# A decoder layer on one core: queries' operands laid out by pairs of heads, maxima issued first at two places, and a context turned by the sync queue

## What is computed

```
x = LN(x + causal_attention(x))            # 16 heads of 16
x = LN(x + slot_attention(x, context))     # see below
x = LN(x + top-4-of-16 experts(x))         # experts of 64

def slot_attention(slots, P):              # 256 slots, 256 rows of context
    Pn = rmsnorm(P, input_norm_w)
    k, v = Pn @ Wk.T, Pn @ Wv.T
    for _ in range(3):
        q = rmsnorm(slots, slot_norm_w) @ Wq.T
        attn = softmax(q @ k.T / 16, axis=slots)
        attn = attn / (attn.sum(-1) + eps)
        slots = gru_cell(attn @ v, slots)
    return slots
```

## Time and profile before

| | us |
|---|---|
| median of 3 runs | 668.17 (667.05 to 669.31) |
| the profiled execution | 666.62 |
| its span in the trace | 664.9 |

### The profile page before, as it was taken

How to read it: one execution, slowest core, us unless ns; L and a number is a source line. 1 busy time by engine, 2 the same in 40 slices (tenths; PEclk the granted TensorE clock), 3 DMA queues, 4 the chain that set the end, 5 groups by cost and what they waited for, 6 DMA issues and landing times.

```text
span 664.9 us, 13964 instructions
## 1 busy us (share of the span) xinstructions
PE 621.7 (93%) x5064; PEld 565.3 (85%) x5064; DVE 493.7 (74%) x1039; ACT 327.0 (49%) x734; POOL 225.2 (34%) x274
## 2 busy tenths in 40 slices
PE   5988998998999999999999999999999998899996
PEld 4766787776767989999899998999989988799996
DVE  4755474674764788879888799887999888767653
ACT  5444553553575355655556555565566644231320
POOL 9402332432453251422223232232312213352543
PEclk9799898997999999999999999999999999999999
DMA  8634646357400040010000000000000000042240
GB/s 283 203 103 146 173 135 190 93 173 217 121 18 1 1 160 0 2 33 2 0 0 0 32 0 0 0 0 0 0 1 1 1 1 1 16 147 82 80 157 34
DMA packets 31374, 43.34 MB, mean 65 GB/s; under 512 B 3072, under 2 KB 18912, under 8 KB 31328
## 3 DMA queue, kind: packets, MB, share of 16 engines
q1 hardware_dynamic: 31328, 42.73, 21.1%
HBM read 29.39 MB, written 13.21 MB: 64 GB/s over the span
## 4 chain that ended last, share of the span: by engine, by line
PE 56%; DVE 13%; issue 13%; DMA 5%; SPq 5%; POOL 4%; ACT 3%; DVEq 0%; POOLq 0%; ACTq 0%
PE bank L448 26%; PE bank L2171 11%; PE bank L1991 4%; POOL hid_hl L801 3%; DMA k_rows<-k_hl 3%; PE bank L1891 2%; DMA q_op<-negT 2%; PE bank L1977 1%; PE bank L456 1%; PE bank L1849 1%; PE bank L2008 1%; SPq L519 1%; PE bank L1856 1%; PE bank L1872 1%; PE bank L2000 1%
## 5 line engine op out<-in xcount | busy, mean ns | idle before, releaser
L448 PE MATMUL bank<-slots_hl,whhT_hl 128*128 128x256 f32 x864 | 113.1, 284 | 0.0
L448 PEld LDWEIGHTS bank<-slots_hl,whhT_hl 128*128 128x128 f32 x864 | 105.5, 188 | 2.4 <-ACT gate_z L1104 1.0
L1293 DVE TENSOR_REDUCE neg_max<-bank 128x2 f32<-128x512 f32 (+1 forms) x96 | 65.7, 690 | 55.2 <-PE bank L1858 41.3
L2171 PE MATMUL bank<-attn_hl,vg_hl 128*128 128x256 f32 x864 | 105.7, 280 | 0.1
L2171 PEld LDWEIGHTS bank<-attn_hl,vg_hl 128*128 128x128 f32 x864 | 100.9, 188 | 4.3 <-ACT attn_hl L815 3.9
L870 ACT ACTIVATE pT<-bank 128x512 f32<-128x512 f32 x96 | 56.9, 598 | 57.7 <-PE bank L1872 41.7
L682 POOL TENSOR_SCALAR_AFFINE_SELECT pT<-pT 128x512 f32<-128x512 f32 x64 | 40.6, 638 | 117.5 <-ACT pT L870 117.4
L696 POOL TENSOR_TENSOR sq<-sq 128x256 f32<-128x256 f32 x24 | 18.1, 754 | 170.6 <-ACT sq L1089 130.3
L801 POOL TENSOR_TENSOR hid_hl<-hid,hid_hl 128x512 fp32r<-128x512 f32 x32 | 40.9, 1303 | 25.8 <-ACT hid_hl L815 25.7
L448 PE MATMUL bank<-x2T_hl,keys_hl 128*128 128x256 f32 x384 | 48.6, 284 | 0.0
L448 PE MATMUL bank<-values_hl,hid_hl 128*128 128x256 f32 x384 | 47.8, 281 | 0.3 <-DVE x L1567 0.3
(11 more groups left out here) (212 smaller groups left out, 1298.2 us busy)
## 6 DMA issues: line engine op xcount, KB each, us to landing
gate_rows<-gate_mem SPq DMA_DIRECT2D x48, 128.0 KB, 3.1
q_rows<-q_hl SPq DMA_DIRECT2D x21, 256.0 KB
k_rows<-k_hl SPq DMA_DIRECT2D x21, 256.0 KB
q_op<-q_rows SPq DMA_DIRECT2D x28, 192.0 KB, 3.2
k_op<-k_rows SPq DMA_DIRECT2D x14, 384.0 KB, 4.4
x_in<-in_x_dram SPq DMA_DIRECT2D x8, 256.0 KB, 6.6
c_in<-in_ctx_dram SPq DMA_DIRECT2D x8, 256.0 KB, 4.8
out_dram<-y_out SPq DMA_DIRECT2D x8, 256.0 KB, 2.8
```

Of the source, the lines that this page charges most:

```text
L448: mm = pe.matmul(dst, left(a), right(b), start=first and n == 0, stop=last and n == 2, skip_group_check=True)
L1293: dve.tensor_reduce(dst, src, AX.X, ALU.max, negate=True).then_inc(max_ok, 1)
L2171: mm = pe.matmul(halves(b)[:, m, :], vg_hl[:, j, v_part, 3 * t + r, q:q + P], attn_hl[:, j, at_part, t, :], start=n == 2 and a + m + t == ...
```

## The change

It has four parts.

1. `q_op` is laid out [partition, batch, pair, head, token], so the two heads of a pair lie side by side and a turned score reads 512 columns in one piece. It and `k_op` have 97 partitions instead of 128, and the memsets and the semaphore for the rows above 97 (`rows_ok`) go. `operands` now brings the queries of one pair's head in a DMA of its own kind: four DMAs of 96 KB with pieces of 1 KB, where there were two of 192 KB with pieces of 2 KB.
2. The maxima are issued first at places 0 and 4, and last as before at places 2 and 6.
3. A second input, `ctxT`, holds the context turned. After the squares of a batch are taken (c_sq) the sync queue overwrites `c_in` with it (`turned_context`), and ACT and DVE make `cT_hl` from there. TensorE's transposes and their banks are gone.
4. `load_context` waits for cT_lo, where it waited for the transposes and the squares.

```diff
-        q_op = sb("q_op", [P, 2, 2, H // 2, T], F32R, where=sq_op)
+        q_op = sb("q_op", [K_ROWS + 1, 2, H // 2, 2, T], F32R, where=sq_op)
...
-            cT, kT, *vg = ((0, 1, 3, 2, 0), (1, 0, 3, 6, 7))[j]
-            jobs = [(("cT", j), cT, cT_lo, 2, 2 + j + 1), (("kT", j), kT, kT_lo, 2, 2 + j + 1)]
+            kT, *vg = ((1, 3, 2, 0), (0, 3, 6, 7))[j]
+            jobs = [(("kT", j), kT, kT_lo, 2, 2 + j + 1)]
...
                 for e in range(2):
-                    sp.dma_start(f32(q_op[48 * e:48 * e + 48, n % 2, e, pairs, :]).rearrange("p q t -> p (q t)"),
-                                 q_rows[n, :, :, :].rearrange("(s e) r w -> e r s w", e=2)[e, :, 2 * half:2 * half + 2, :]
-                                 ).then_inc(ops_in[n % 2][half], 16)
+                    for s in range(2 * half, 2 * half + 2):
+                        sp.dma_start(f32(q_op[48 * e:48 * e + 48, n % 2, 2 * s:2 * s + 2, e, :]),
+                                     q_rows[n, 2 * s + e, :, :].rearrange("r (c t) -> r c t", c=2)).then_inc(ops_in[n % 2][half], 16)
...
+            def turned_context(i, j):
+
+                sp.wait_ge(c_sq, due(2, i, j + 1))
+                sp.sem_inc(passed, 1)
+                sp.dma_start(c_in[:, j, :, :], rows(ctxT[i * 2 + j, :, :], NC)).then_inc(cT_arr[j], 16)
...
+                if quad in (QUADS - 6, QUADS - 5):
+                    turned_context(0, quad - (QUADS - 6))
+                if place in (0, 4) and 0 <= quad // 2 + 1 < 2 * B:
+                    maxima(quad // 2 + 1)
                 if place == 0:
...
-                if quad % 2 == 0 and 0 <= quad // 2 + 1 < 2 * B:
+                if place in (2, 6) and 0 <= quad // 2 + 1 < 2 * B:
                     maxima(quad // 2 + 1)
...
                 for j in range(2):
 
-                    sp.wait_ge(cT_mm, due(2, i, j + 1, back=1))
-                    sp.sem_inc(passed, 1)
-                    sp.wait_ge(c_sq, due(2, i, j + 1, back=1))
+                    sp.wait_ge(cT_lo, due(2, i, j + 1, back=1))
                     sp.sem_inc(passed, 1)
                     sp.dma_start(c_in[:, j, :, :], ctx[i * 2 + j, :, :].rearrange("(t p) d -> p t d", p=P)).then_inc(c_arr[j], 16)
+                for j in range(2):
+                    turned_context(i, j)
...
-            for e in range(2):
-                pool.memset(f32(q_op[K_ROWS:, 0, e, :, :]), 0.0).then_inc(rows_ok, 1)
-            pool.wait_ge(rows_ok, 2)
...
-                act.wait_ge(cT_mm, due(2, r, 2 + j + 1))
+                act.wait_ge(cT_arr[j], due(1, r, 2, step=16))
                 act.wait_ge(vg_mm, due(6, r, 6 + 3 * j))
-                copy(cT_hl[:, HI, :, :], halves(context_bank(("cT", j), first))).then_inc(cT_hi, 1)
+                copy(cT_hl[:, HI, :, :], c_in[:, j, :, :]).then_inc(cT_hi, 1)
...
                 if third < 2:
-                    mm = pe.matmul(halves(b), k_op[:, n % 2, pair_of(quad, third), 0:P],
-                                   q_op[:, n % 2, :, pair_of(quad, third), :], start=True, stop=True)
+                    mm = pe.matmul(bank[b][:, :], k_op[:, n % 2, pair_of(quad, third), 0:P],
+                                   q_op[:, n % 2, pair_of(quad, third), :, :].rearrange("p e t -> p (e t)"), start=True, stop=True)
```

More of the change, by code:

```diff
@@ L66, in after, with decoder_layer @@
         engine.wait_ge(signal, count)
-def decoder_layer(nc, x, xT, ctx, w_qkv, w_proj, wq, wk, wv, wihT, whhT, eselT, keys, values, cols, lines, out):
+def decoder_layer(nc, x, xT, ctx, ctxT, w_qkv, w_proj, wq, wk, wv, wihT, whhT, eselT, keys, values, cols, lines, out):
     stack = ExitStack()
@@ L155, in decoder_layer @@
         x_in = sb("x_in", [P, 2, NT, D], where=s1)
-        k_op = sb("k_op", [P, 2, H // 2, T], F32R, where=s1)
+        k_op = sb("k_op", [K_ROWS + 1, 2, H // 2, T], F32R, where=s1)
         v_aug = sb("v_aug", [P, 3, NT, H, 2 * DH], where=s1)
@@ L284, in decoder_layer @@
         c_sq, c_mean, c_rstd, c_kept = event("c_sq", 2), event("c_mean", 2), event("c_rstd", 2), event("c_kept", 1)
-        cT_mm, cT_hi, cT_lo = event("cT_mm", 2), event("cT_hi", 2), event("cT_lo", 2)
+        cT_arr = [event(f"cT_arr{j}", 1, 16) for j in range(2)]
+        cT_hi, cT_lo = event("cT_hi", 2), event("cT_lo", 2)
         kT_mm, kT_hi, kT_lo = event("kT_mm", 2), event("kT_hi", 2), event("kT_lo", 2)
@@ L858, in set_queries @@
                     act.wait_ge(set_mm, 3 * s + e + 1)
-                    copy(q_op[0:K_ROWS, 0, e, 2 * s:2 * s + 2, :], halves(set_bank(s, e))[0:K_ROWS, :, :]).then_inc(set_q, 1)
+                    copy(q_op[0:K_ROWS, 0, 2 * s:2 * s + 2, e, :], halves(set_bank(s, e))[0:K_ROWS, :, :]).then_inc(set_q, 1)
             def maxima_out(hh):
@@ L1346, in context_text_lo @@
                 dve.wait_ge(cT_hi, due(2, r, 2 + j + 1))
-                sub_hi(cT_hl[:, LO, :, :], halves(context_bank(("cT", j), first)), cT_hl[:, HI, :, :]).then_inc(cT_lo, 1)
+                sub_hi(cT_hl[:, LO, :, :], c_in[:, j, :, :], cT_hl[:, HI, :, :]).then_inc(cT_lo, 1)
             def context_keys_lo(r, j, first=False):
@@ L1848, in natural @@
                         for e in range(2):
-                            pe.matmul(bank[b][:, (2 * c + e) * P:(2 * c + e + 1) * P], q_op[0:K_ROWS, n % 2, e, pair_of(quad, c), 0:P],
+                            pe.matmul(bank[b][:, (2 * c + e) * P:(2 * c + e + 1) * P], q_op[0:K_ROWS, n % 2, pair_of(quad, c), e, 0:P],
                                       k_op[0:K_ROWS, n % 2, pair_of(quad, c), 0:P], start=c + e == 0, stop=False, skip_group_check=True)
@@ L1855, in natural @@
                     for e in range(2):
-                        pe.matmul(halves(b)[:, e, :], q_op[0:K_ROWS, n % 2, e, pair_of(quad, c), P:],
+                        pe.matmul(halves(b)[:, e, :], q_op[0:K_ROWS, n % 2, pair_of(quad, c), e, P:],
                                   k_op[0:K_ROWS, n % 2, pair_of(quad, c), :], start=e == 0, stop=False, skip_group_check=True)
@@ L1876, in turned @@
                         mm = pe.matmul(halves(b)[:, c, :].rearrange("p (e n) -> p e n", e=2), k_op[:, n % 2, pair_of(quad, c), P:],
-                                       q_op[:, n % 2, :, pair_of(quad, c), P:], start=c == 0, stop=c == 1, skip_group_check=True)
+                                       q_op[:, n % 2, pair_of(quad, c), :, P:], start=c == 0, stop=c == 1, skip_group_check=True)
                 mm.then_inc(t_mm, 1)
@@ L1944, in free_bank @@
                 return b
-            def context_text(r, j, first=False):
-                b = free_bank(r, ("cT", j), first)
-                pe.wait_ge(c_arr[j], due(1, r, 2, step=16))
-                transpose4(pe, b, lambda t, c: c_in[:, j, t, c * P:(c + 1) * P]).then_inc(cT_mm, 1)
             def context_keys(r, j, first=False):
@@ L2024, in first_context @@
             def first_context(quad):
[L2026 to L2028 removed]
+                if quad == QUADS - 3:
                     context_keys(-1, 0, True)
```

34 lines of the change are left out of this document (12 added, 22 removed).

## The result

The changed kernel took **688.1 us** (median of 4 runs, 687.2 to 690.0) against 667.6 for the kernel before in the same comparison (666.9 to 669.3): ratio 1.031 (95% interval 1.028 to 1.034), 20.8 us slower. The sign was forecast, the size was not: 674.5 with a range of 664 to 682.

What follows compares the result with a forecast made beforehand. In attention the in-order sync queue and its DMAs were taken to set the end. Losses 1.0 + 3.5 + 3.5 + 2.9 = 10.9 us against gains of 3.9, net +7.0, gave 674.5 us, range 664 to 682.

Steps and rivals of the forecast that it cites:

- Maxima first at places 0 and 4: Attention's sync queue: operands and rows wait for negT at place 0; 3.0 us per stall in quads 8 to 23.
- Queries' operands in four DMAs instead of two: Operands calls on the sync queue: 0.4 us per extra issue, 0.8 before place 2's maxima, taken as 0.5 a stall.
- The piece of 1 KB at 0: Query DMAs: pieces of 1 KB instead of 2 KB cost nothing in landing; at most 2.4 us over three stalls.
- A new stall in the last period: Scores of quad 30: late k_op operands stall TensorE 1.9 us, plus 1.0 for clock, in all 2.9 us.
- Turned scores that read one piece: TensorE's turned scores in attention: no gain, since starts are already close; ends 0 and 1.3 us, 7.8 as a rival.
- rival C: Turned scores: the duration difference is real TensorE time, 7.8 us, giving 666.7 us; chance 0.05.
- Context turned by the queue: TensorE loses eight transpose groups: 2.2 us in the loop, 1.0 for the scales' bank, 0.7 after; gain 3.9 us.
- A: Attention: the queue's wait at place 0 is swallowed and only the gains stand, 664.3 us; chance 0.15.
- B: Attention: slack takes most of the delay, losses 4 against gains 3.9, a draw at 668.3 us; chance 0.10.
- D: Attention: longer stalls also delay operands of place 2 and quads 14 and 22, 680 us; 0.08 of the forecast's 0.70.
- The ends of the range: Whole kernel: forecast's own range, 667.5 us (losses 5.7, gains 4.6) to 680.5 (losses 15.2, gains 3.0, plus 1.5).
- a fixed price of clock per stall: TensorE in attention: a stall lowers the granted clock afterwards; 1.0 us added for the last period's new stall.

Runs made afterwards that it cites:

- e11: Kernel before with the maxima issued first at place 0 only, nothing else; 677.8 us, ratio 1.0159.
- e13: Kernel before with two more DMAs of 32 bytes in each operands call, ahead of the keys' piece, into a tile nobody reads; 670.9 us, ratio 1.0065.
- e3: Kernel before with only the new layout of the queries' operands and its four DMAs; 681.0 us, ratio 1.0194.
- e4: Kernel before with only the context turned by the queue; 661.8 us, ratio 0.9948.
- e6: Kernel before, old layout and 2 KB pieces kept, each query DMA of 192 KB cut in two of 96 KB; 672.6 us, ratio 1.0119.
- e7: Kernel before with the maxima issued first at place 2 only, last elsewhere; 666.8 us, ratio 1.0009.
- e15: Kernel before with maxima first at place 2, context by the queue, second keys' rows write moved from place 3 to 5, behind place 4's maxima; 652.2 us, 0.9781.
- e17: Changed kernel, with its layout, four query DMAs and context by the queue, but the queue's order of e15; 665.9 us, ratio 0.9989.

## Why the prediction was right or wrong

- **"Maxima first at places 0 and 4"**: right in mechanism and nearly in size. Its terms without the DMAs' share came to 9.1 us; measured 11.0 (6.4 to 15.7). The place is right too: 10.6 at place 0, nothing at place 4. The prediction took 3.0 of 3.9 us of lateness to reach the keys' rows. In e11 the operands start at 92.51 (87.52 before) and the next ones at 106.70 (102.53): 4.2 of 5.0 us. So the slack that it allowed for, 0.9 us, is about what there was, and the lateness was larger.
- **"Queries' operands in four DMAs instead of two"**: this is the step that failed. It gave 0.5 us to each of the two stalls of quads 8 to 23 and, in the four pieces priced at 1.6 us, 0.8 to the last period: 1.8 of the sum. Measured 12.9 (7.4 to 18.5). Three things were mis-sized in it. An issue was priced at 0.4 us, taken from the DMAs of before with their 2 KB pieces; the new ones with 1 KB pieces take 0.60, and the keys' issue behind them 0.59 instead of 0.43, so a call grows by 1.87 us and not 0.8. It was counted once a stall, while two calls stand ahead of the maxima of place 2. And it was then cut from 0.8 to 0.5, on the ground that the DMA engines and not the issues might set the landing; e13 shows that issues that move next to nothing cost time too. With 6 x 1.87 = 11.2 us in its place, the sum would have been 9.1 + 11.2 - 3.9 = 16.4 us against 20.8. That 11.2 is near 12.9 is partly luck: the waits grew by 9.2 in e3, and nothing in 11.2 stands for a lower clock.
- **The piece of 1 KB at 0**: consistent with the table above, not proven.
- **"A new stall in the last period"**: there, 2.70 us at 205.30 where I had 1.9. That the stalls would otherwise stand at the maxima was wrong. Some 14 us of waits for them were forecast, the longest about 6; they came to 10.7, the longest 4.0, and 16.6 us stand at the scores, the longest 6.4, for the keys' piece, which is issued last of five. The changed calls at place 2 land so late that TensorE stops there first.
- **"Turned scores that read one piece"**: right. The duration is 535 ns against 526, the starts are as before (e3 above), and rival C is out.
- **"Context turned by the queue"**: 3.9 predicted, 3.5 measured (1.2 to 5.8), right in total. In the loop the copies of the context follow one another at 368.76 and 451.04 us in the kernel before, 82.28 us a pair, and at 367.97 and 449.24 in e4, 81.27. So 1.0 a pair, as predicted (1.07). But the 1.0 for the scales' bank was not gained: the wait for vg_hl took its place at 0.9 us. The saving beyond the 0.72 of two groups lies in what follows them: the twelve products behind the first batch's group take 1.36 us by starts (366.12 to 367.48 in e4) instead of 1.50 (367.27 to 368.77), those behind the second's 1.49 instead of 1.67 without the wait. In that part the total is right by luck. Why they start closer without transposes ahead of them, no run shows.
- **Rivals.** A and B counted on slack in the DMA engines and fell. D, 680 us by longer stalls elsewhere, had the right kind of mechanism with 0.08 of the chance. What pushed the time past the range was the one term above: without the 11.1 us that it was short, 688.1 would be 677.0.
- **The ends of the range** are off by 0.2 us each as sums: 666.6 + 5.7 - 4.6 is 667.7, and 666.6 + 15.2 - 3.0 + 1.5 is 680.3. Nothing hangs on it.

The Trainium skill, Perfetto Trace Analysis, What "DMA-bound" means, says that a kernel can be bound by the sequencer that issues its DMAs, and not only by the DMA engines, and knows it by a track of solid issues. The trace agrees for stretches: from 87.52 to 97.44 us the sync queue of the kernel before issues without a gap of 0.3 us, and then it waits for 5 us; and in e13 two issues a call of 0.28 us and 32 bytes cost 4.3 us. The Trainium skill, Perfetto Trace Analysis, DMA Optimizations, adds that smaller DMAs may let a task end sooner where the DMA engines are generally idle. The runs bound that: with the DMA engines at a mean share of 0.43 from 50 to 218 us, the halved DMAs of e6 landed in 2.4 us instead of 3.2, and the kernel lost 7.9 us.

## What to carry to other kernels

Price a DMA on the queue that issues it, per issue and by its own shape, and multiply by every call that stands ahead of the transfer that is waited for, not by the number of stalls. In a queue that takes its work in order, put a DMA that waits for a late result where the queue would idle anyway (place 2 here), never ahead of transfers that are ready; then look at what the next backlog delays, since the first such move gained nothing (e7) until the bulk write behind it was moved too (e15). Parts of a change are worth timing alone: here 3.5 us of gain lay hidden under 24 of loss, and another order of the same queue, worth 10.7 us, was two moves away from the kernel before. A part that costs through one wait need not become free when that wait is gone: the layout cost as much under the better order (e17).

## What was not expected of the hardware

- **The price of an issue depends on its shape and its neighbours.** This is a row of e3 and one of the kernel before (duration ns least, median, most); then the copies of the context in e4 and before, on which the point above rests:

```profile
L506 SPq DMA_DIRECT2D q_op<-q_rows x56: 572/596/1582, 28.2 to 190.3; - x56
```

```profile
L506 SPq DMA_DIRECT2D q_op<-q_rows x28: 308/424/1268, 27.3 to 176.7; - x28
```

```profile
367.97 0.62 ACT L823 ACTIVATE cT_hl<-c_in 128x512 fp32r<-128x512 f32 x1
...
449.24 0.62 ACT L823 ACTIVATE cT_hl<-c_in 128x512 fp32r<-128x512 f32 x1
```

```profile
368.76 0.59 ACT L815 ACTIVATE cT_hl<-bank 128x512 fp32r<-128x512 f32 x1
...
451.04 0.59 ACT L815 ACTIVATE cT_hl<-bank 128x512 fp32r<-128x512 f32 x1
```

  A 32-byte DMA took 0.28 us. The keys' issue, the same DMA each time, took 0.59 us behind the DMAs with 1 KB pieces, 0.43 behind those with 2 KB pieces, and 0.33 behind the small ones. In places an issue took up to 1.6 us: four of them 4.99 at 107.38 in e17. That a backlog of the DMA engines does this is a guess; no run separates it.
- **The granted clock is down before the stall is over.** In the changed kernel TensorE stood still until 116.85 us, 5.53 us in all. The clock was 1.00 from 113 to 114 us; this row, wholly inside the stall, has 0.50, which is the 1.2 GHz level. It was back at 1.00 from 125 us on.

```profile
115.00:116.00 1.00, 0.00 (x0) 0.00 (x0) 0.00 (x0) 0.00 (x0) 0.00 (x0) 0.50 0.82 279
```

- **Not every stall costs clock.** The first stall of the kernel before, 1.78 us to 67.31, was followed by 0.66 in the stretch of 67 to 72 us; the first of e13, 2.24 us to 67.12, by 1.00 in the same stretch. In e17 the stall to 86.39 (1.54 us) was followed by 0.83 over ten us, the one to 153.39 (1.71 us) by 1.00. So a fixed price of clock per stall, as the prediction and e7's expectation have it, is a guess, and single executions of like kernels differ by it: e13's attention ended at 214.56 us, 0.9 ahead of the kernel before, with 2.3 us more of waits.
- The kernel before spread over 662 to 670 us on other chips than its first comparison, where it kept within 667 to 669. From the last copy of the context in the loop to the end it took 664.9 - 461.2 = 203.7 us in its profiled execution, and the same part took 207.2 in e4 (666.1 - 458.9). The difference arises behind the loop, in the experts' part: from the start of one and the same group of products there (564.19 and 561.40) to the end it took 100.7 and 104.7. So part of the spread comes from there, and single profiled spans of two kernels can't be told apart within 4 us.
